# A window-attention block on one core: SyncE's transfers of a step begin only behind the second band's scores of the following step

## The chip, the cores and the metric

One Trainium2 chip, one of its cores. The metric is the time on the device in microseconds (us), the median over runs. The engines are called as in the profile: PE is TensorE's matmul, PEld its weight load, DVE is VectorE, ACT is ScalarE, POOL is GpSimd, SP is SyncE and SPq the queue in which it issues DMAs.

## The reference

A shifted-window attention block with its MLP, all in float32, on x of shape 32 x 56 x 56 x 128 (32 images), with 4 heads of 32 and windows of 7 x 7 tokens:

```
h   = layernorm(x, g1, b1); roll by (-3, -3); cut into 7x7 windows
q, k, v = split(h @ w_qkv + b_qkv)
a   = softmax(q k^T / sqrt(32) + rel_bias + mask)      # per window and head
x   = x + roll_back(unwindow((a v) @ w_proj + b_proj))
out = x + gelu(layernorm(x, g2, b2) @ w_fc1 + b_fc1) @ w_fc2 + b_fc2
```

## The kernel before

**Tiling.** A step is two bands of 7 image rows, 784 tokens, laid out as 112 partitions (two bands of 56 columns) x 7 tiles x 128 channels. An image has 4 steps, so there are 128 steps (`steps`), numbered through. The roll by 3 is done by the DMAs: a step's load is 6 DMAs, and 9 for every fourth step, which wraps round the image's end; its store is the same number of DMAs. `x_in` and `stream` in SBUF have 4 slots (STEPS), and step k uses slot k % 4. `x_in` holds the loaded x. `stream` holds the running result of the step: POOL first writes x plus the projection's bias into it (`add_row` with `x_in`, signal `x_biased`), DVE adds the projection (`residual_added`), POOL adds the second MLP bias, DVE adds the MLP's product in two halves (`out_added[0]`, `out_added[1]`), and SyncE stores it.

**The order is written out by hand.** Each engine runs its own program, a function `step(n)` called for n from -3 to 129 (`run_steps`). One call of it works on several steps of the data at once: in PE's `step(n)` are the projection of n, the scores of n+1 (band 0 near its beginning, band 1 in its middle), most of the MLP of n-1 and its product with w_fc2, the transposes of the first layer norm of n+2, the transposes of the second layer norm xn2 of n, and the attention product of n+1. Engines take their instructions strictly in this order and are tied by semaphores; `upto(k)` is the count that a semaphore with one signal per step has once step k is done, and at most the count of the last step, so `wait(sp, scores_made[1], upto(n + 1))` asks for the scores of the second band of step n+1. A wait for a count of zero or less is left out.

**The pieces around the change.**
- SyncE's `step(n)` (L282 to L293): the load of step n+4 into the slot of step n, after `x_biased` and both halves of `xn1_ready` of n, then the store of step n-2, after both halves of `out_added` of n-2. Loads of steps 0 to 3 and of the weights stand ahead of the loop.
- POOL's `step(n)` (L324 to L343), in this order: normalise the probabilities of n-1, both bands (L314); second MLP bias of n-2 (L321, on `stream`); the power for the first layer norm of n+2 (`rstd1`, L318); x plus bias of n+1 (L321, from `x_in`), which waits for the load of n+1 and for the store of n-3, whose slot it writes over; the power for the second layer norm of n-1 (`rstd2`, L318).
- DVE's `step(n)` (L601 to L661): ...; bias, maximum and shift of the scores of n, band 1, once `scores_made[1]` of n is signalled (L568 to L573); row sums of band 0; then xn2 of n-1, first half (L553, needs `rstd2`); `out_added[0]` of n-2 (L587); row sums of band 1; `out_added[1]` of n-2; the split of x2T and the second half of xn2; the statistics of x of n+3 (L532, needs its load); and more.
- PE's `step(n)` (L768 to L866): `make_scores(1)` of n+1 at L808 signals `scores_made[1]` (L690); then transposes, `make_out(0)`, `make_q`, `make_out(1)` (L763); then the wait for `out_added[0]` of n-1 and the transposes of xn2 of n (L695), and the rest of the step.

Of the kernel before, what the change touches and what calls it, by code (L numbers as in the profile page):

```python
# [42 lines left out]
def wait(eng, sem, value):  # L43

    if value > 0:
        eng.wait_ge(sem, value)

def swin_block(nc, x, g1, b1, w_qkv, b_qkv, w_proj, b_proj, rel_slices, g2, b2, w_fc1, b_fc1, w_fc2,
# [4 lines left out]
    def has(k):  # L53

        return 0 <= k < steps

    def upto(k):

        return min(k, steps - 1) + 1

    def run_steps(step):
        for n in range(-LEAD, steps + LAG):
            step(n)

    with ExitStack() as ctx:
# [92 lines left out]
        def sems(name, n=2):  # L158
            return [sem(f"{name}{i}") for i in range(n)]
# [32 lines left out]
        scores_made = sems("scores_made")  # L192
# [37 lines left out]
        def token_pieces(s, dram, img, tile):  # L230

            pieces = []
            for band in range(BANDS):
                row = STEP_ROWS * s + WIN * band + SHIFT
                whole = min(WIN, ROWS - row)
                for first, t0, t1 in ((row, 0, whole), (0, whole, WIN)):
                    if t0 < t1:
                        rows = dram[img, first * COLS:(first + t1 - t0) * COLS, :].rearrange("(t p) c -> p t c", p=COLS)
                        for col, p, n in ROLLED:
                            p += COLS * band  # L240
                            pieces.append((rows[col:col + n, :, :], tile[p:p + n, t0:t1, :]))
            assert len(pieces) == LOADS[s]
            return pieces

        def dma_count(s, img):

            return img * (16 * LOADS[s]) + 16 * LOADS[s]

        def load_rel(eng, half):

            eng.wait_ge(rel_cleared, 1)
            for ni in range(WIN):
                p, i0 = HALF * half + WIN * ni, WIN - 1 - ni
                eng.dma_start(rel[p:p + WIN, :, :],
                              rel_slices[:, half, :, i0:i0 + WIN, :].rearrange("q h i j -> q h (i j)")).then_inc(rel_loaded, 16)
# [3 lines left out]
        @block.sync  # L259
        def _(sp):  # L260
            def load(img, s):
                for src, dst in token_pieces(s, x, img, x_in[:, s, :, :]):
                    sp.dma_start(dst, src).then_inc(x_loaded[s], 16)

            def store(img, s):
                for dst, src in token_pieces(s, out, img, stream[:, s, :, :]):
                    sp.dma_start(dst, src).then_inc(out_stored[s], 16)

            load(0, 0)
            for dst, src in ((wqkv[:, :], w_qkv), (vecs[:, 0:1], g1), (vecs[:, 1:2], b1), (vecs[:, 2:3], g2),  # L270
                             (vecs[:, 3:4], b2), (bqkv[:, :], b_qkv), (wproj[:, :], w_proj),
                             (wfc1_raw[:, :], w_fc1), (bfc1[:, :], b_fc1),
                             (wfc2[:, :, :], w_fc2.rearrange("(k p) n -> p k n", p=C)),
                             (brow_proj_in[:, :], b_proj.to_broadcast([TOK, C])),
                             (brow_fc2[:, :], b_fc2.to_broadcast([TOK, C])),
                             (mask_sb[:, :, :, :], mask)):
                sp.dma_start(dst, src).then_inc(weights_loaded, 16)
            load_rel(sp, 0)
            for s in range(1, STEPS):
                load(0, s)  # L280

            def step(n):  # L282
                if has(n) and has(n + STEPS):

                    wait(sp, x_biased, upto(n))
                    wait(sp, xn1_ready[0], upto(n))
                    wait(sp, xn1_ready[1], upto(n))
                    load((n + STEPS) // STEPS, n % STEPS)
                if has(n - 2):

                    wait(sp, out_added[0], upto(n - 2))
                    wait(sp, out_added[1], upto(n - 2))
                    store((n - 2) // STEPS, (n - 2) % STEPS)  # L293

            run_steps(step)

            for s in range(STEPS):
                sp.wait_ge(out_stored[s], dma_count(s, images - 1))
# [621 lines left out]
```

## Time and profile before

| | |
|---|---|
| median of 3 runs | 3122.12 us (3111.51 to 3128.21) |
| the profiled execution | 3099.51 us, its span 3097.7 us |
| busy share PE / DVE / ACT / POOL | 97% / 90% / 74% / 42% |
| mean granted clock of TensorE | 0.992 |
| SyncE's transfers | 104.14 MB on queue q1, 13.2% of 16 DMA engines' time |
| SyncE's longest wait in total | for DVE's stream L587 (out_added), 2391.3 us in 128 waits |

The table is read as shares of one long span in which nearly all steps are alike; what sets the time of a step has to be read from the timeline of one of them. The granted clock is a share of 2.4 GHz: 1.00 is that level and 0.50 is 1.2 GHz.

### The profile page before, as it was taken

What the parts mean: (1) busy time and instruction counts of PE and PEld (TensorE: products, weight loads), DVE (VectorE), ACT (ScalarE), POOL (GpSimd) and SP (SyncE); (2) the same over time, 40 slices, a digit from 0 to 9 for tenths busy, and PEclk for the clock granted to TensorE, in tenths of its full rate; (3) what the DMA queues carried; (4) which work ended last, traced back from release to release, by engine and by line L of the source; (5) the groups of instructions that cost most, each with busy time, mean ns of one, the idle gap of its engine ahead of it and who ended that gap; (6) DMA issues with size and microseconds to landing.
All of it is one profiled execution on the core that took longest, in us unless ns stands there. A gap on an engine that the chain in (4) does not pass through costs nothing.

```text
span 3097.7 us, 119627 instructions
## 1 busy us (share of the span) xinstructions
PE 3003.0 (97%) x51984; PEld 2725.4 (88%) x51984; DVE 2803.2 (90%) x7463; ACT 2305.0 (74%) x4482; POOL 1306.6 (42%) x775
## 2 busy tenths in 40 slices
PE   5999999999999999999999999999999999999998
PEld 3898888989988898998899889988999888998897
DVE  7899988999989899999999999989999899999994
ACT  4777777777777777777777777777777777777774
POOL 2444444444434444444444444444444344444442
PEclk8999999999999999999999999999999999999999
DMA  1111111111111111111111111111111111111100
GB/s 55 34 34 34 44 34 34 33 44 34 34 33 44 34 34 35 43 34 33 44 33 34 40 37 34 36 41 34 34 39 39 33 34 39 39 33 37 41 18 22
DMA packets 217572, 111.81 MB, mean 36 GB/s; under 512 B 15094, under 2 KB 216790, under 8 KB 217046
## 3 DMA queue, kind: packets, MB, share of 16 engines
q1 hardware_dynamic: 216899, 104.14, 13.2%
q8 instruction: 408, 6.68, 0.9%
q14 instruction: 118, 0.97, 0.1%
q10 hardware_dynamic: 147, 0.02, 0.0%
HBM read 52.73 MB, written 51.38 MB: 34 GB/s over the span
## 4 chain that ended last, share of the span: by engine, by line
PE 59%; DVE 38%; issue 2%; ACT 0%; SPq 0%; DMA 0%; POOL 0%; POOLq 0%; ACTq 0%; DVEq 0%
PE psum L721 11%; DVE xn L553 9%; PE psum L722 7%; PE psum L723 7%; PE psum L688 7%; DVE row_sum L580 7%; PE psum L742 7%; PE psum L749 6%; PE psum L716 6%; DVE stream L587 4%; DVE scores L568 4%; DVE row_max L571 4%; DVE scores L573 4%; PE psum L703 4%; PE psum L695 3%; DVE x2T_lo L598 2%
## 5 line engine op out<-in xcount | busy, mean ns | idle before, releaser
L763 PEld LDWEIGHTS psum<-wfc,hT 128*112 128x112 f32 x7168 | 806.1, 177 | 39.2 <-issue 21.5
L763 PE MATMUL psum<-wfc,hT 128*112 128x128 f32 x7168 | 824.1, 273 | 1.5 <-ACT hT L407 1.5
L407 ACT ACTIVATE hT<-psum,bias_h 128x392 f32<-128x392 f32 x1024 | 578.8, 594 | 314.6 <-PE psum L723 301.7
L318 POOL TENSOR_TENSOR rstd<-ve,minus_half 112x7 f32<-112x7 f32 x256 | 381.1, 1489 | 986.7 <-DVE ve L548 986.7
L314 POOL TENSOR_TENSOR probs<-probs,row_inv 128x784 f32<-128x784 f32 x256 | 388.7, 1519 | 689.8 <-DVE row_inv L582 689.8
L553 DVE TENSOR_SCALAR xn<-stream,mean,rstd 112x128 f32<-112x128 f32 x896 | 460.4, 571 | 1.6 <-POOL rstd L318 1.6
L587 DVE TENSOR_TENSOR stream<-psum,stream 112x512 f32<-112x512 f32 (+1 forms) x512 | 305.6, 606 | 169.7 <-PE psum L749 153.0
L721 PE MATMUL psum<-x2T_hi,wfc_hi 128*128 128x392 f32 x1024 | 405.0, 395 | 9.2 <-DVE x2T_lo L598 2.0
L722 PE MATMUL psum<-x2T_hi,wfc_lo 128*128 128x392 f32 x1024 | 351.9, 344 | 12.4 <-issue 12.4
L723 PE MATMUL psum<-x2T_lo,wfc_hi 128*128 128x392 f32 x1024 | 351.9, 344 | 0.0
L394 ACT ACTIVATE qd<-psum,bias_q,parity_one 128x392 f32<-128x392 f32 x512 | 316.9, 669 | 3.3 <-PE psum L723 3.3
L321 POOL TENSOR_TENSOR stream<-stream,brow_fc 112x896 f32<-112x896 f32 x128 | 269.0, 2102 | 93.5 <-DVE xn L553 93.5
L721 PEld LDWEIGHTS psum<-x2T_hi,wfc_hi 128*128 128x128 f32 x1024 | 193.5, 189 | 106.5 <-DVE x2T_lo L598 87.4
L695 PE MATMUL psum<-ident,xn 112*128 112x112 f32 x1792 | 271.3, 268 | 10.6 <-DVE xn L553 9.1
L568 DVE TENSOR_TENSOR scores<-psum,bias_rel 128x784 f32<-128x784 f32 x256 | 247.2, 966 | 34.3 <-PE psum L688 34.2
L321 POOL TENSOR_TENSOR stream<-x_in,brow_proj 112x896 f32<-112x896 f32 x128 | 270.3, 2112 | 0.5 <-DMA out<-stream 0.5
L742 PE MATMUL psum<-wv,xT 128*113 128x128 f32 x2048 | 265.4, 272 | 0.0
L573 DVE TENSOR_TENSOR scores<-scores,row_max 128x784 f32<-128x784 f32 x256 | 249.5, 975 | 8.7
L571 DVE TENSOR_REDUCE row_max<-scores 128x16 f32<-128x784 f32 x256 | 248.3, 970 | 8.8
L353 ACT ACTIVATE probs<-scores 128x784 f32<-128x784 f32 x256 | 223.7, 874 | 42.5 <-DVE scores L573 41.1
L361 ACT ACTIVATE probsT<-psum 128x452 f32<-128x452 f32 x512 | 252.0, 550 | 0.6 <-PE psum L703 0.6
L389 ACT ACTIVATE x2T_hi<-psum 128x448 fp32r<-128x448 f32 (+1 forms) x256 | 127.5, 498 | 166.7 <-PE psum L695 166.6
(78 smaller groups left out, 5663.2 us busy)
## 6 DMA issues: line engine op xcount, KB each, us to landing
x_in<-in_x SPq DMA_DIRECT2D x224, 168.0 KB
out<-stream SPq DMA_DIRECT2D x224, 168.0 KB
x_in<-in_x SPq DMA_DIRECT2D x224, 17.5 KB
out<-stream SPq DMA_DIRECT2D x224, 17.5 KB
x_in<-in_x SPq DMA_DIRECT2D x224, 10.5 KB
out<-stream SPq DMA_DIRECT2D x224, 10.5 KB
x_in<-in_x SPq DMA_DIRECT2D x32, 96.0 KB
out<-stream SPq DMA_DIRECT2D x32, 96.0 KB
```

What stands on the lines that cost most here:

```text
L314: pool.tensor_tensor(p, p, r.unsqueeze(2).to_broadcast([128, 2 * WINDOWS, N]), ALU.mult).then_inc(probs_normed[band], 1)
L318: pool.tensor_tensor(rstd[:, :], ve[:, :], minus_half[:, :], ALU.pow).then_inc(ready, 1)
L321: pool.tensor_tensor(stream[:, k % STEPS, :, :], src[:, k % STEPS, :, :], row[:, :].unsqueeze(1).to_broadcast([TOK, TILES, C]), ALU.add).t ...
L407: act.activation(hT[:, chunk, band * BAND:(band + 1) * BAND], tok_psum(c)[:, 0:BAND], ACT.Gelu, bias=bias_h[:, chunk:chunk + 1]).then_inc( ...
L553: last = dve.tensor_scalar(dst[:, t, :], src[:, t, :], mean[:, t:t + 1], rstd[:, t:t + 1], ALU.subtract, ALU.mult)
L573: dve.tensor_tensor(rows, rows, mx.unsqueeze(2).to_broadcast([128, 2 * WINDOWS, N]), ALU.subtract).then_inc(scores_shifted[band], 1)
L587: dve.tensor_tensor(s, tok_psum(h)[0:TOK, 0:(t1 - t0) * C], s, ALU.add).then_inc(ready[h], 1)
L721: pe.matmul(made, w_hi, x_hi, start=True, stop=False)
L722: pe.matmul(made, w_lo, x_hi, start=False, stop=False)
L723: return pe.matmul(made, w_hi, x_lo, start=False, stop=True)
L742: last = pe.matmul(qkvo_psum(V_BANK[band])[0:rows, pair * C:(pair + 1) * C], windows[:, 0:rows], wv[:, :], start=True, stop=True)
L763: last = pe.matmul(tok_psum(h)[0:TOK, (t - t0) * C:(t - t0 + 1) * C], hT[:, chunk, t * TOK:(t + 1) * TOK], wfc2[:, chunk, :], start=chunk ...
```

## The change

SyncE gets one more wait at the head of its `step(n)`, ahead of the load's waits and of the store's. It stands there in every call, whether the call issues something or not. All other engines' programs, the DMAs and the buffers are as before.

```diff
             def step(n):
+                wait(sp, scores_made[1], upto(n + 1))
                 if has(n) and has(n + STEPS):
 
                     wait(sp, x_biased, upto(n))
```

## Rows read from the trace of the kernel before

**Rows 1.** The page's first part: busy us, share of the span, instructions.
```profile
PE 3003.0 (97%) x51984; PEld 2725.4 (88%) x51984; DVE 2803.2 (90%) x7463; ACT 2305.0 (74%) x4482; POOL 1306.6 (42%) x775
```

**Rows 2.** Timeline, PE, one step: start us, us, engine, line, operation [idle before].
```profile
1509.48 0.95 PE L688 MATMUL psum<-kT,qd 64*49 64x49 f32 x64
...
1517.49 0.60 PE L695 MATMUL psum<-ident,xn 112*128 112x112 f32 x4
...
1533.18 0.95 PE L688 MATMUL psum<-kT,qd 64*49 64x49 f32 x64
```

**Rows 3.** Timeline, POOL and DVE in the same step.
```profile
1504.67 2.11 POOL L321 TENSOR_TENSOR stream<-x_in,brow_proj 112x896 f32<-112x896 f32 x1
...
1510.29 1.49 POOL L318 TENSOR_TENSOR rstd<-ve,minus_half 112x7 f32<-112x7 f32 x1 [3.51 <-DVE ve L548]
...
1514.56 2.27 DVE L553 TENSOR_SCALAR xn<-stream,mean,rstd 112x128 f32<-112x128 f32 x4
...
1516.76 0.68 DVE L587 TENSOR_TENSOR stream<-psum,stream 112x512 f32<-112x512 f32 x1
...
1520.72 1.44 DVE L532 BATCH_NORM_STATS2 raw<-x_in 112x6 f32<-112x128 f32 x7
```

**Rows 4.** Timeline, POOL: the bias add of steps 4, 5 and 126.
```profile
103.64 2.11 POOL L321 TENSOR_TENSOR stream<-x_in,brow_proj 112x896 f32<-112x896 f32 x1
...
126.93 2.11 POOL L321 TENSOR_TENSOR stream<-x_in,brow_proj 112x896 f32<-112x896 f32 x1
...
2990.26 2.11 POOL L321 TENSOR_TENSOR stream<-x_in,brow_proj 112x896 f32<-112x896 f32 x1
```

**Rows 5.** Timeline, SyncE's queue: two steps' stores (L267) and loads (L263).
```profile
1495.79 3.29 SPq L267 DMA_DIRECT2D out<-stream  x9
1499.18 2.13 SPq L263 DMA_DIRECT2D x_in<-in_x  x6
1519.09 2.27 SPq L267 DMA_DIRECT2D out<-stream  x6
1521.47 3.18 SPq L263 DMA_DIRECT2D x_in<-in_x  x9
```

**Rows 6.** Timeline near the end: a store, and the bias add behind it.
```profile
3004.66 3.27 SPq L267 DMA_DIRECT2D out<-stream  x9
...
3009.06 2.39 POOL L321 TENSOR_TENSOR stream<-x_in,brow_proj 112x896 f32<-112x896 f32 x1 [0.51 <-DMA out<-stream]
```

**Rows 7.** Windows: us, busy of PE, PEld, DVE, ACT, POOL, PEclk, DMA share, GB/s.
```profile
1502.50:1503.00 0.50, 0.50 (x5) 0.49 (x4) 0.43 (x5) 0.50 (x2) 0.00 (x0) 1.00 0.08 13
```

**Rows 8.** Windows near the beginning, columns as before.
```profile
40.00:42.00 2.00, 0.28 (x1) 0.28 (x2) 1.93 (x3) 1.67 (x4) 0.00 (x0) 0.50 0.00 0
```

**Rows 9.** Timeline, PE, near the beginning.
```profile
41.72 1.68 PE L728 MATMUL psum<-xT,wqk 128*128 128x392 f32 x2 [5.50 <-ACT vs L403]
```

**Rows 10.** Timeline, PE, two gaps inside otherwise steady work.
```profile
410.81 0.41 PE L716 MATMUL psum<-probsT,vs 49*32 49x49 f32 x12 [2.96 <-issue]
...
411.96 0.53 PE L723 MATMUL psum<-x2T_lo,wfc_hi 128*128 128x392 f32 x1
...
909.69 0.38 PE L716 MATMUL psum<-probsT,vs 49*32 49x49 f32 x4 [2.81 <-issue]
```

**Rows 11.** Timeline, POOL: the bias adds around these two gaps.
```profile
411.55 2.09 POOL L321 TENSOR_TENSOR stream<-x_in,brow_proj 112x896 f32<-112x896 f32 x1
439.25 2.11 POOL L321 TENSOR_TENSOR stream<-x_in,brow_proj 112x896 f32<-112x896 f32 x1
...
910.51 2.10 POOL L321 TENSOR_TENSOR stream<-x_in,brow_proj 112x896 f32<-112x896 f32 x1
939.51 2.11 POOL L321 TENSOR_TENSOR stream<-x_in,brow_proj 112x896 f32<-112x896 f32 x1
```

**Rows 12.** Timeline, PE's weight loads in the step of rows 2.
```profile
1519.60 0.19 PEld L721 LDWEIGHTS psum<-x2T_hi,wfc_hi 128*128 128x128 f32 x1 [0.68 <-DVE x2T_lo L598]
...
1522.97 1.27 PEld L716 LDWEIGHTS psum<-probsT,vs 49*32 49x32 f32 x128 [0.33 <-issue]
```

## The prediction

> **What bounds the kernel now.** I read the page's busy line first: TensorE is busy for 97% of the span, DVE for 90% [rows 1]. Neither has room to make up for much, so anything that holds either of them once per step may be paid in full. Then I read the timeline of one step in the middle of the run, and there the order at a single point matters. PE makes the second band's scores and ends them at 1509.48 + 0.95 = 1510.43 [rows 2]; it goes on with other work and starts the transposes of xn2 at 1517.49, with no idle time noted before them. DVE normalises xn2 from 1514.56, with no idle time before it, and adds the first half of the finished step to the stream at 1516.76 + 0.68 = 1517.44, which is what those transposes wait for (out_added[0]) [rows 3]. The reader is to see that DVE reaches this point 0.05 us before PE needs it: whatever makes DVE's xn2 late makes PE late by as much. The steady step is 126.93 - 103.64 = 23.29 us, and over the 122 steps from 103.64 (slot work of step 4) to 2990.26 (step 126) the mean is 2886.62 / 122 = 23.66 us [rows 4]; the 0.37 us between them are PE's stalls for which the profile names "issue" and steps such as the two discussed below.
>
> **What the change moves.** In SyncE's step n the new wait comes before all else. It asks for the second band's scores of step n+1, made in the middle of PE's step n. Behind it on SyncE stand the load of n+4 and the store of n-2. In the trace of before that same store (the one that follows a finished out_added[1]) goes out at 1495.79 and the load behind it at 1499.18, while the scores that the new wait asks for end at 1510.43 [rows 2, 5]. The store thus moves from 1495.79 to behind 1510.43, and a load now stands ahead of it, since the step's load precedes its store.
>
> Who waits for these two? The load feeds x statistics. With the scores of step n+1 made at 1510.43, the load of n+4 is issued by about 1513.7; its first consumer is DVE's statistics at 1520.72 [rows 3], which will themselves be later. The load is hidden, with over 5 us to spare against any landing in the rows. The store feeds POOL. POOL's step n+1 waits for the store of n-2 before it writes x plus the bias of n+2 over the same stream slot, the operation at 1504.67 (2.11 us); the next one in POOL's order is rstd2 at 1510.29 (1.49 us) [rows 3]. And DVE waits for that rstd2 before it normalises xn2, in the same step in which it used the very scores the new wait names. So the order is now forced: scores made, load issued, store issued, store landed, POOL's bias add, POOL's rstd2, DVE's xn2, DVE's out_added[0], PE's transposes. Before, the bias add was over 3.6 us before the scores were (1506.78 against 1510.43) and hid behind everything. Behind the bias add on POOL are also the two normalisations of the probabilities, but these need DVE results that come after or together with xn2, so they keep their distance to it.
>
> **The sum of one step**, from the end of the scores to the start of DVE's xn2. SyncE released, 0.10 (an estimate: nearest is the gap of 0.11 between its store and its load below, in which it passes three waits that are already met). The load's 6 issues, 2.13; in one step of four there are 9, 3.18. Gap to the store, 0.11 (1519.09 + 2.27 to 1521.47). The store's 6 issues, 2.27; one step in four 9, 3.29 [rows 5]. From the end of the issues to POOL's start, 1.13: at the tail, the only place where POOL does wait for a store today, the 9 issues end at 3004.66 + 3.27 = 3007.93 and POOL starts at 3009.06 [rows 6]. Bias add, 2.11, and rstd2, 1.46 more (its 1.49 begins 0.03 before the other's end) [rows 3]. DVE's start, 0.05. Sum 0.10 + 2.13 + 0.11 + 2.27 + 1.13 + 2.11 + 1.46 + 0.05 = 9.36 us for 6 + 6 issues. Loads of 9 go with stores of 6 and the reverse, so two steps in four have 15 issues: about 10.38 us. The mean is 9.87. Before, the same stretch was 1514.56 - 1510.43 = 4.13 us [rows 2, 3]. The stall is 5.2 or 6.3 us, **mean 5.74**.
>
> Does anything take it back? DVE has nothing else to do meanwhile, its queue is in order; and PE has work until about 1517.5 and then nothing, its queue is in order too. From xn2's start on, DVE's and POOL's work has the same relative times as before, and PE's from 1517.49 to the next scores' end at 1533.18 + 0.95 = 1534.13 is nearly solid [rows 2]. I book nothing back. The first store stands in step 2 and POOL first waits for it for slot 4's bias add, the last for 127's: **124 stalls**, 124 x 5.74 = 712 us. The start and the end of the run stay as they are: after the last scores the new wait is already met, and the weights' loads are ahead of it.
>
> The uncertain terms: the landing. The lowest that rows allow is 1.13; a load of 6 issued from 1499.18 to 1501.31 still shows a DMA share of 0.08 between 1502.50 and 1503.00, so 1.7 is the upper end [rows 5, 7]; that would add 0.57 x 124 = 70 us. I take the row where POOL really waited, 1.13. DMA: Bandwidth & Descriptors, in the section Anatomy of one DMA — SWDGE (gpsimd) path of the Trainium skill, gives a fixed cost of about 2.0 us per DMA, mostly the receipt of the write; that path is not SyncE's, but counted from the last issue's start it would put the landing near the upper end and my time some 70 us up, an estimate.
>
> **The clock.** PE will now sit idle for 5.2 to 6.3 us in each step. The trace has short and long gaps of PE to price this by. PE waited 5.50 us ahead of 41.72, and the granted clock is 0.50 there, the 1.2 GHz level [rows 8, 9]. Even a gap of 2.96 us in the middle of solid work (ahead of 410.81) was followed by matmuls of 0.53 us, and that step took 439.25 - 411.55 = 27.70 us: 4.41 over 23.29, of which 2.96 less the usual 0.33 is the gap, so the clock cost 1.8 us [rows 10 to 12]. The gap of 2.81 ahead of 909.69 made its step 939.51 - 910.51 = 29.00: 5.71 over, less 2.48, so 3.2 us. Both gaps are half of what is coming; I therefore expect the low clock after every stall. Bounds are nothing and 3.2 us; of the cost some is absorbed, because right behind the transposes PE has waits for DVE and POOL that would shrink (one is the weight load's 0.68 us for x2T_lo [rows 12]). I take **1.6 us**, a little below the smaller of the two prices. 124 x 1.6 = 198 us.
>
> Total: 712 + 198 = 910 us on the profiled time of 3099.51, 4010 us. The median of the runs is 22.6 us above the profiled one, so the forecast against it is 3122 + 910 = 4032, rounded to **4030 us**, 29% slower. The step should be 23.66 + 7.34 = 31.0 us.
>
> **Rivals.**
> (a) The stall is there but the clock stays at 2.4 GHz, or its loss is wholly absorbed: 3122 + 712 = 3834 us. For it: the waits behind the transposes. Against it: gaps half as long were enough to bring the clock down. TensorE: Matmul & The Clock Gate, HAM oscillation — how this bites in real kernels, in the Trainium skill, describes a loop in which one DMA wait per pass throttles the array anew each time and half of the throttled time is lost; by it this rival is out. By that rule the trace agrees for a single gap, the one ahead of 410.81 [rows 10]; a gap in every step no row of before shows.
> (b) The clock costs as much as in the dearer of the two cases, 3.2 us, every time: 3122 + 712 + 397 = 4231 us. For it: PE resumes with a mix of short work and waits. Against: absorption.
> (c) Only a part of the stall reaches PE, because some of PE's later waits vanish with it or the POOL operations run faster beside an idle DVE: half of 712 and no clock, about 3480 us. Against: no idle time of PE in [rows 2] that depends on anything ahead of the stall.
> (d) The other side: the store's delay is still covered, and moving the DMA traffic away from the stretch of the attend matmuls takes PE's stalls "issue" away (such as the 0.33 us ahead of L716 [rows 12]). At most the 0.37 us per step between 23.66 and 23.29 would go: 3122 - 122 x 0.37 = 3077 us. It decides only if the chain from the store to rstd2 ends before DVE asks for it at 1514.56, so the store would have to have landed by 1514.56 - 3.6 = 1511.0, half a microsecond behind the scores. It can do that only if the new wait is met earlier than I read it, that is, if it asked for scores of a step already past; by the same misreading the change would do nothing.
> (e) The load, not the store, is late and stops DVE at its statistics. That needs a landing over 10 us after the scores plus the stall itself. No row is near; it would add to the time, not replace the stall. I give it no chance of its own.
>
> **How the numbers follow.** Forecast 0.60 (its own range 3940 to 4120, from landing 1.13 to 1.7 and clock 1.2 to 1.9), (a) 0.15, (b) 0.17, (c) 0.05, (d) with "nothing changes" 0.03. The range 3840 to 4220 leaves out (c), (d) and the outer parts of (a) and (b). Faster by over 0.5% has 0.015, within 0.5% (about what a measurement of this kernel can tell) 0.015, slower 0.97.
>
> **What the changed profile would show.** SyncE's waits lead with PE's scores L688 as releaser instead of DVE's stream L587. SyncE's timeline has load and store back to back, 12 or 15 issues, once per step, just behind the second scores. POOL's bias add L321 waits for DMA out<-stream some 124 times, and the distance from the scores' end to it is about 6 to 7 us. DVE's xn L553 on the stream waits for rstd L318, 5 to 6 us a time; PE's transposes L695 wait for DVE's stream L587 about as long. The granted clock falls to some 0.85 or less on the mean. The bias-add period is about 31 us. Wrong would be: L553 without a wait (then (c) or (d)), a granted clock near 0.99 (then (a)), or statistics L532 waiting for the load (then (e)).

## The result and the profile after

| | median us | lowest and highest of 5 runs |
|---|---|---|
| before | 3122.12 | 3111.51 to 3128.21 |
| changed | 4138.76 | 4130.57 to 4147.73 |
| ratio | 1.3285 | 95% interval 1.3243 to 1.3328 |

The changed kernel takes 1017 us more, a third. The forecast was 4030 us with a range of 3840 to 4220.

The page of the changed kernel begins as follows (busy time by engine, then the chain that ended last). The added line moves all line numbers behind it up by one, so L689 here is L688 before, L322 is L321, L554 is L553.

```profile
PE 3257.6 (79%) x51984; PEld 2982.0 (72%) x51984; DVE 2801.9 (68%) x7463; ACT 2338.7 (56%) x4482; POOL 1295.2 (31%) x775
...
PE 56%; SPq 14%; POOL 11%; DVE 10%; DMA 6%; issue 4%; ACT 0%; POOLq 0%; ACTq 0%; DVEq 0%
```

DVE's busy time is the same as in [rows 1] to within 2 us and POOL's is 11 us less, so neither got more work. PE is busy 255 us longer with the same 51984 instructions: that is a slower clock, not work. And the chain that ended last now runs through SyncE's queue, POOL and the DMAs for 31% of the span; in the kernel before, the page gives each of them 0% of it.

The waits, in total, and SyncE's own (engine, line <- what it waited for: us, times, longest):

```profile
POOL stream L322 <- DMA out<-stream: 1661.6, 124, 18.6
...
DVE xn L554 <- POOL rstd L319: 796.1, 126, 8.0
PE psum L696 <- DVE stream L588: 790.7, 125, 8.0
```
```profile
SPq L263 <- PE psum L689: 3264.0, 123, 31.3
```

POOL's bias add waits for the store 124 times, the number counted in the prediction, and the two waits behind it have the same size, 790.7 / 125 = 6.33 us each: what DVE loses for rstd2, PE loses for DVE. The 1661.6 us of POOL are longer because POOL comes to its wait early; they are not the price.

One step of the changed kernel, the same instructions as in [rows 2] and [rows 3] (timeline: start us, us, engine, line, operation, idle before it; SyncE's queue and POOL's among them, lines of other work left out):

```profile
2005.43 0.95 PE L689 MATMUL psum<-kT,qd 64*49 64x49 f32 x64
...
2006.44 2.13 SPq L263 DMA_DIRECT2D x_in<-in_x  x6
...
2008.67 3.56 SPq L267 DMA_DIRECT2D out<-stream  x9
...
2013.36 2.07 POOL L322 TENSOR_TENSOR stream<-x_in,brow_proj 112x896 f32<-112x896 f32 x1 [12.70 <-DMA out<-stream]
2015.38 1.49 POOL L319 TENSOR_TENSOR rstd<-ve,minus_half 112x7 f32<-112x7 f32 x1
...
2016.91 2.30 DVE L554 TENSOR_SCALAR xn<-stream,mean,rstd 112x128 f32<-112x128 f32 x4 [6.31 <-POOL rstd L319]
2019.14 0.68 DVE L588 TENSOR_TENSOR stream<-psum,stream 112x512 f32<-112x512 f32 x1
...
2019.87 1.01 PE L696 MATMUL psum<-ident,xn 112*128 112x112 f32 x4 [6.28 <-DVE stream L588]
```

Read it as a staircase. The scores end at 2006.38, SyncE issues 0.06 us later, load and store are out at 2012.23, POOL starts 1.13 us behind, DVE gets its rstd2 at 2016.87, PE its go at 2019.82. Each step of the stair begins within 0.1 us of the end of the one above but for the landing. From the scores' end to DVE's xn2 there are 10.53 us, where there were 4.13.

The four transposes that end the list are listed with 1.01 us; the same ones take 0.60 in [rows 2]. The clock around them (windows: length, busy PE, PEld, DVE, ACT, POOL, PEclk, DMA share, GB/s):

```profile
2018.00:2020.00 2.00, 0.13 (x1) 0.13 (x2) 2.00 (x6) 0.00 (x0) 0.36 (x1) 0.50 0.00 0
2020.00:2022.00 2.00, 2.00 (x12) 2.00 (x13) 1.86 (x4) 0.87 (x2) 0.95 (x1) 0.50 0.00 0
2022.00:2024.00 2.00, 2.00 (x7) 1.37 (x6) 2.00 (x9) 1.02 (x3) 1.32 (x2) 0.53 0.00 0
2024.00:2026.00 2.00, 2.00 (x21) 1.97 (x20) 0.53 (x3) 1.81 (x4) 1.35 (x1) 1.00 0.00 0
```

PE sat idle, and when it resumed the granted clock stood at 0.50, the 1.2 GHz level, for about 4 us of full work. The clock records show a stretch at the lower level in each of 120 steps counted from xn2 to xn2, where the kernel before has one in 5 of 120; the mean clock of the span is 0.876 against 0.992.

The period of the bias add, to be set beside [rows 4] (steps 4 and 126, 122 steps apart):

```profile
118.61 2.07 POOL L322 TENSOR_TENSOR stream<-x_in,brow_proj 112x896 f32<-112x896 f32 x1 [13.05 <-DMA out<-stream]
...
4038.50 2.08 POOL L322 TENSOR_TENSOR stream<-x_in,brow_proj 112x896 f32<-112x896 f32 x1 [9.83 <-DMA out<-stream]
```

(4038.50 - 118.61) / 122 = 32.13 us, against 23.66: 8.47 us per step. PE's wait for DVE's stream, averaged over the 121 steps that the timeline shows whole, is 6.41 us of it. That leaves 2.06 us, for which the low clock is the suspect. (By the delay of xn2, 10.66 us behind the scores on the mean against 4.13, the stall is 6.53 us and the remainder 1.94: the listed idle time of PE starts at the modelled end of its last matmul, about 0.1 us late. The experiments below go by the listed idle time.)

### The profile page after: what moved, and what is told of

Same layout as the page of the kernel before. It is cut to its first block, busy times and chain, and to the rows that moved or that the text cites. A ratio compares the mean times of both kernels' runs of the same rounds, so it can differ in the third digit from the quotient of the medians.

```text
span 4145.9 us, 119751 instructions
## 1 busy us (share of the span) xinstructions
PE 3257.6 (79%) x51984; PEld 2982.0 (72%) x51984; DVE 2801.9 (68%) x7463; ACT 2338.7 (56%) x4482; POOL 1295.2 (31%) x775
## 4 chain that ended last, share of the span: by engine, by line
PE 56%; SPq 14%; POOL 11%; DVE 10%; DMA 6%; issue 4%; ACT 0%; POOLq 0%; ACTq 0%; DVEq 0%
PE psum L704 8%; PE psum L722 7%; DVE xn L554 7%; SPq L263 7%; SPq L267 7%; POOL stream L322 6%; PE psum L723 6%; PE psum L724 6%; PE psum L689 5%; DMA out<-stream 5%; PE psum L743 5%; PE psum L696 5%; PE psum L750 5%; POOL rstd L319 4%; PE psum L717 4%; PE psum L729 4%
## 5 line engine op out<-in xcount | busy, mean ns | idle before, releaser
L554 DVE TENSOR_SCALAR xn<-stream,mean,rstd 112x128 f32<-112x128 f32 x896 | 438.9, 546 | 795.7 <-POOL rstd L319 795.7
L696 PE MATMUL psum<-ident,xn 112*128 112x112 f32 x1792 | 321.6, 305 | 800.6 <-DVE stream L588 790.7
L696 PEld LDWEIGHTS psum<-ident,xn 112*128 112x128 f32 x1792 | 223.8, 162 | 834.5 <-DVE stream L588 815.8
L322 POOL TENSOR_TENSOR stream<-x_in,brow_proj 112x896 f32<-112x896 f32 x128 | 265.0, 2070 | 1661.6 <-DMA out<-stream 1661.6
L722 PE MATMUL psum<-x2T_hi,wfc_hi 128*128 128x392 f32 x1024 | 473.3, 462 | 3.4 <-DVE x2T_lo L599 2.0
L723 PE MATMUL psum<-x2T_hi,wfc_lo 128*128 128x392 f32 x1024 | 364.8, 356 | 9.9 <-issue 9.9
L704 PE MATMUL psum<-ident,probs 113*128 113x113 f32 x2048 | 363.3, 344 | 2.2 <-POOL probs L315 2.2
L724 PE MATMUL psum<-x2T_lo,wfc_hi 128*128 128x392 f32 x1024 | 363.4, 355 | 0.0
L704 PEld LDWEIGHTS psum<-ident,probs 113*128 113x128 f32 x2048 | 335.1, 198 | 12.4 <-POOL probs L315 3.7
L729 PE MATMUL psum<-xT,wqk 128*128 128x392 f32 x512 | 296.9, 673 | 9.9 <-ACT vs L404 7.9
L362 ACT ACTIVATE probsT<-psum 128x452 f32<-128x452 f32 x512 | 270.2, 550 | 61.1 <-PE psum L704 59.8
L322 POOL TENSOR_TENSOR stream<-stream,brow_fc 112x896 f32<-112x896 f32 x128 | 268.3, 2096 | 93.4 <-DVE xn L554 93.4
```

The source lines that it names most:

```text
L322: pool.tensor_tensor(stream[:, k % STEPS, :, :], src[:, k % STEPS, :, :], row[:, :].unsqueeze(1).to_broadcast([TOK, TILES, C]), ALU.add).t ...
L554: last = dve.tensor_scalar(dst[:, t, :], src[:, t, :], mean[:, t:t + 1], rstd[:, t:t + 1], ALU.subtract, ALU.mult)
L696: last = pe.transpose(tok_psum(h)[:, (t - t0) * TOK:(t - t0 + 1) * TOK], src[:, t, :], ident[0:TOK, 0:TOK])
L704: last = pe.transpose(psum[:, S_BANK + 2 * band + f, 128 * pair:128 * pair + rows], probs[0:rows, band, f, 2 * pair:2 * pair + 2, :].rearr ...
L722: pe.matmul(made, w_hi, x_hi, start=True, stop=False)
L723: pe.matmul(made, w_lo, x_hi, start=False, stop=False)
```

## Experiments

The theory to be tested: the store lands late, POOL's in-order queue puts rstd2 behind the bias add that waits for it, DVE and PE lose 6.4 us, and the idle PE loses its clock for another 2 us. Its rivals: the load is what comes late; a wait in SyncE's queue, or the meeting of its traffic with other work, costs by itself; the remainder of 2 us is not the clock.

**1. The store ahead of the load, behind the same wait.**

```diff
                 wait(sp, scores_made[1], upto(n + 1))
-                (load of n+4) (store of n-2)
+                (store of n-2) (load of n+4)
```

> The changed kernel with the store placed ahead of the load behind the same wait. Theory (store landing, POOL's bias add, rstd2, DVE's xn2, PE): the load's issues leave the chain, 2.57 + 0.11 = 2.7 us per step of the changed kernel, so the stall falls from 6.4 to about 3.7 us and the time to 4139 - 124 x 2.7 = 3805 us, less if the clock falls more rarely. Rival (the load is what arrives too late): it now goes out later, so no gain or a loss, 4139 us or more.

Measured: 3805.19 us, ratio 1.2197 (1.2146 to 1.2247). From the waits:

```profile
DVE xn L554 <- POOL rstd L319: 453.6, 126, 4.6
PE psum L696 <- DVE stream L588: 447.8, 125, 4.5
```

The time is the expected one. The load, issued later still, made nothing slower, and the stall fell by 2.81 us, to 3.60 us on the mean: the load's issues and the gap behind them took 2.64 us of the chain, and the store's own issues take 0.16 us less when no load stands right ahead of them. The period is 29.23 us, so what is left over the stall, 29.23 - 23.66 - 3.60 = 1.97 us, is as large as with the longer gap. A gap of 3.6 us costs as much clock as one of 6.4. The clock records show why: the time at the lower level falls from some 1030 us in the changed kernel to 667, but the part of it in which PE has work hardly changes, 622 and 598 us. What the longer gap adds at the low clock is time in which PE is idle anyway.

**2. Only the load gated; the store goes out ahead of the wait.**

```diff
+                (store of n-2)
                 wait(sp, scores_made[1], upto(n + 1))
                 (load of n+4)
-                (store of n-2)
```

> Only the load stands behind the new wait, the store goes out ahead of it as before. Theory: nothing waits for the load, so the time is that of the kernel before, 3122 us within 0.5%. Rival (the late load stalls DVE's statistics, or the wait's place or the meeting of load traffic with other work costs by itself): over 3200 us.

Measured: 3104.36 us, ratio 0.9959 (0.9936 to 0.9982). The load as the culprit is out: it is delayed as in the changed kernel and costs nothing. Whether the 0.4% is a gain is taken up in 7 and 8.

**3. PE kept busy in its wait, twice.** Behind the last of the MLP's product and ahead of the wait for out_added[0], PE gets matmuls whose result nothing reads, in columns of a PSUM bank that nothing uses. They are added work, the rest is computed as before.

```diff
+            def fill(count):
+                for _ in range(count):
+                    pe.matmul(psum[:, QKVO_BANK + 1, BAND:512], ident[:, :], wfc2[:, 0, 0:512 - BAND], start=True,
+                              stop=True)
...
                     make_out(1)
                 if has(n):
+                    if n >= 2:
+                        fill(44)
                     wait(pe, out_added[0], upto(n - 1))
```

> The changed kernel with 44 idle matmuls (120 columns into columns of a PSUM bank that nothing reads) ahead of PE's wait for out_added[0], from step 2 on: some 5 us of work that fits into the wait of 6.4 us, so the gap is about 1.3 us. The stall itself stays. Theory (of the 8.4 us per step 6.4 are the stall and 2.0 the low clock behind it): the mean granted clock goes to 0.97 or more and the time to about 4139 - 124 x 2.0 = 3890 us. Rival (the remainder is not the clock but other waits): 4139 us or, for the added work, more.

Measured: 4303.78 us, ratio 1.38 (1.375 to 1.3851), clock 0.99. I had sized the filler wrongly: the 44 took 9.98 us instead of some 5, more than the gap, so PE no longer waited at all and its own filler became the bound. The run says that the clock stays up when PE has work, and nothing of the price. With half as many:

> The changed kernel with 22 idle matmuls ahead of PE's wait for out_added[0]. With 44 they took 9.98 us, more than the wait, so 22 take 5.0 us and fit into the wait of 6.4 us, leaving a gap of 1.4 us. The stall itself stays. Theory (6.4 us per step are the stall, 2.0 us the low clock behind it): mean granted clock 0.97 or more, 4139 - 124 x 2.0 = 3890 us. Rival (the remainder over the stall is not the clock): 4139 us.

Measured: 3942.13 us, ratio 1.2661 (1.2623 to 1.2698), clock 0.982. In the timeline (each of the 22 matmuls is recorded as two instructions):

```profile
2010.22 5.07 PE L762 MATMUL psum<-wfc,ident 128*128 128x120 f32 x44
...
2016.86 0.60 PE L696 MATMUL psum<-ident,xn 112*128 112x112 f32 x4 [1.57 <-DVE stream L588]
```

DVE's wait for rstd2 is unchanged (789.8 us against 796.1), so the stall is the same, filled with useless work; the transposes are back at 0.60 us, and the kernel is 197 us faster for it. Per step, by the period of the bias add, 32.13 - 30.45 = 1.68 us. As the clock has two levels, 1.00 and 0.50, the time at the lower one is twice the missing share of the span: 2 x 0.124 x 4145.9 = 1028 us in the changed kernel, 2 x 0.018 x 3947.0 = 142 us here, 2 x 0.008 x 3097.7 = 50 us in the kernel before. So at least 1.7 of the 2.06 us are the clock, and 30.45 - 23.66 - 6.40 = 0.39 us per step are left. The same trace says what they are. Counted from xn2 to xn2, 93 of 120 steps have no time at the low level; their period is 30.00 us and DVE's wait for rstd2 6.46, which leaves 23.54 us, against 23.47 in the 115 such steps of the kernel before. The other 27 steps take 31.96 us. The remainder is thus the clock that still fell in these, and 0.39 x 124 = 48 us of it are nearly all of the 52 us by which the time is above the expected one.

**4. POOL's bias add one step later, out of the way of rstd2.**

```diff
             (POOL, step(n))
                 if has(n - 2):
                     wait(pool, xn2_ready[1], upto(n - 2))
                     add_row(n - 2, stream, brow_fc2, x1_biased)
+                if has(n):
+                    wait(pool, x_loaded[n % STEPS], dma_count(n % STEPS, n // STEPS))
+                    if has(n - 4):
+                        wait(pool, out_stored[n % STEPS], dma_count(n % STEPS, (n - 4) // STEPS))
+                    add_row(n, x_in, brow_proj, x_biased)
                 (rstd1 of n+2)
-                (the same for n + 1, with its two waits)
                 (rstd2 of n-1)
             (DVE, step(n))
                     wait(dve, proj_made[0], upto(n))
+                    wait(dve, x_biased, upto(n))
                     add_to_stream(n, 0, residual_added)
```

> The changed kernel, but POOL adds x and the bias of a step one step later, behind the second bias add, so that neither rstd2 nor the probabilities stand behind the wait for the store; DVE gets a wait for x_biased ahead of the first half of the projection. Theory: the store has landed 5 us or more before POOL asks for it, nobody waits, 3122 us within 1%. Rival (the late transfers cost by traffic or through another consumer): over 3200 us.

Measured: 3133.81 us, ratio 1.0051 (1.0027 to 1.0074). The wait of POOL for the store is gone from the waits, and with it all but 0.5% of the loss, though SyncE's transfers are as late as in the changed kernel, the load 0.06 us behind the scores' end at 1504.81:

```profile
1503.86 0.95 PE L690 MATMUL psum<-kT,qd 64*49 64x49 f32 x64
...
1504.87 2.13 SPq L263 DMA_DIRECT2D x_in<-in_x  x6
1507.10 2.43 SPq L267 DMA_DIRECT2D out<-stream  x6
```
```profile
1517.48 2.11 POOL L322 TENSOR_TENSOR stream<-x_in,brow_proj 112x896 f32<-112x896 f32 x1
```

The bias add begins 7.95 us after the store is out (1509.53) and with no idle time. This is the whole mechanism undone at its narrow place, not at SyncE. The control is the same edit on the kernel before:

> The kernel before with POOL's later bias add alone: the control for the changed kernel with it. Theory: nobody waits for that operation in either, so this is 3122 us within 1% and equal to the other (3134 us) within 0.5%. Rival (the changed order of SyncE costs some of the 14 us there): below 3120 us.

Measured: 3137.16 us, ratio 1.0072 (1.0046 to 1.0099), the same as with the change within 0.1% by the medians and 0.2% by the ratios. So the 0.5 to 0.7% belong to POOL's new order, and with that order SyncE's new wait costs nothing that can be measured. The two traces agree: their steps without low clock take 23.67 and 23.71 us, where those of the kernel before take 23.47.

**5. The wait on the first band's scores, 5.0 us earlier.**

```diff
-                wait(sp, scores_made[1], upto(n + 1))
+                wait(sp, scores_made[0], upto(n + 1))
```

> The changed kernel with the wait on the first band's scores of the same step, which end 5.0 us earlier. Theory: the chain from the scores to DVE's xn2 starts 5.0 us earlier, so of the mean stall of 6.4 us 1.4 us are left (1.1 for 12 issues, 1.7 for 15), the gap is too short to bring the clock down each time, and the time is 3122 + 124 x 1.4 = 3298 us. Rival (any wait in the middle of PE's step costs most of the loss): over 3600 us; rival (slack I have not seen): 3122 us.

Measured: 3450.92 us, ratio 1.1079 (1.1041 to 1.1116). Two thirds of the loss are gone, but the number is 153 us above my expectation. The waits:

```profile
POOL stream L322 <- DMA out<-stream: 1046.0, 124, 12.5
...
PE psum L696 <- DVE stream L588: 250.7, 125, 3.1
```

The stall is 250.7 / 125 = 2.0 us, not 1.4, because the chain from the first band's scores to xn2 takes 11.3 us here, where the chain behind the second band's took 10.66. POOL's two operations now meet DVE's score arithmetic, and both sides are slower for it:

```profile
1503.27 2.08 POOL L322 TENSOR_TENSOR stream<-x_in,brow_proj 112x896 f32<-112x896 f32 x1 [7.67 <-DMA out<-stream]
1503.39 2.80 DVE L574 TENSOR_TENSOR scores<-scores,row_max 128x784 f32<-128x784 f32 x1
...
1505.31 2.22 POOL L319 TENSOR_TENSOR rstd<-ve,minus_half 112x7 f32<-112x7 f32 x1
```

On the mean rstd2 takes 1.85 us instead of 1.49, the bias add 2.21 instead of 2.07, and DVE's shift of the second band's scores 1.71 instead of 0.97 (that of the first band, which meets neither, stays at 0.97); DVE is thus itself later at xn2 and waits for rstd2 only 159.5 / 124 = 1.3 us. The landing is longer too, 1.86 us on the mean instead of 1.64; why was not tested. And the clock falls in about half of the steps (62 of 120; mean 0.960; 276 us at the low level), which I had ruled out for gaps so short. The period is 26.56 = 23.66 + 2.03 + 0.87. To see whether the 0.87 us are the clock, the same with 8 idle matmuls in the gap:

> The changed kernel with the wait on the first band's scores (3451 us where 3298 was expected), and 8 idle matmuls, some 1.8 us, ahead of PE's wait for out_added[0], which took 2.0 us there. If that miss is a stall of 2.0 instead of 1.4 us plus 0.87 us per step of low clock, the gap all but vanishes, the clock stays up (0.985 or more) and the time is 3451 - 124 x 0.87 = 3343 us. If the miss is anything but the clock: 3451 us.

Measured: 3385.69 us, ratio 1.0867 (1.0838 to 1.0897), clock 0.990: 65 us faster with more work in it. In the trace the period falls by 0.65 us to 25.92. The clock is most of the 0.87 us and not all of it. In the 111 of 120 steps without low clock the period is 25.65 us, 2.18 above the 23.47 of such steps before, where the stall accounts for 2.03: 0.15 us are not clock and weren't separated. The time is 43 us above the expected one.

**6. The wait one step earlier.**

```diff
-                wait(sp, scores_made[1], upto(n + 1))
+                wait(sp, scores_made[1], upto(n))
```

> The changed kernel with the wait on the second band's scores of one step earlier, which are made over 8 us before the store's own wait is met. Theory: the wait instruction costs nothing by itself, 3122 us within 0.5%. Rival (an added wait in SyncE's queue costs by itself): slower by over 1%.

Measured: 3102.22 us, ratio 0.9957 (0.9935 to 0.998). The wait as such is free; its price is the event it names.

**7 and 8. Is there a gain in 2 and 6?** Both came out 0.4% below the kernel before, with intervals clear of 1, and neither had a shorter period in its trace (23.68 and 23.71 us against 23.66). So they were run again beside an unchanged copy of the kernel before.

> The kernel before, unchanged, as the null for the two runs below: a ratio of 1.000, and how far one build of the same program lies from another.

> Only the load behind the new wait, again. The first time it was 0.4% faster with an interval clear of 1, and its period in the trace was the same 23.66 us. If moving the load away helps: 0.996 again. If it was the spread between runs: 1.000, within 0.3%.

> The wait one step earlier, again; also 0.4% faster the first time, though nothing is moved in it. 1.000 within 0.3% if that was spread; 0.996 again if the added wait by itself shifts something.

Measured: the unchanged copy 1.0023 (1.0007 to 1.0039), the gated load 0.9972 (0.9955 to 0.9989), the earlier wait 0.9973 (0.9957 to 0.9989). The copy, which can't differ, differs from itself by 0.2%, beyond its own interval. Against the copy the two are 0.5 and 0.6% lower, against the other runs 0.3%. What differs with the time is the granted clock: its median over the runs is 0.9865 for the copy, 0.988 for the other runs of the kernel before, and 0.9895 and 0.990 for the two. Among the runs of the kernel before alone it goes the same way, 3130.39 us at 0.983 and 3098.64 at 0.991. The steps without low clock take 23.40 us with the gated load and 23.41 with the earlier wait, 23.45 and 23.51 in the first runs of the two, 23.47 and 23.52 in the kernel before and its copy. So a gain of that size can't be told from the spread between runs, which comes with how often the clock falls; what makes it fall more or less often isn't shown. I leave it open. No version was found that clearly beats the kernel before.

## Why the prediction was right

The measured median lies 109 us above the forecast, inside the stated range, but 19 us above the forecast's own narrower range of 3940 to 4120. By the number alone it is nearer to rival (b), 4231, than to 4030, so it is the steps that decide. By the prediction's own steps:

- **DVE reaches its point 0.05 us before PE needs it, so DVE's delay is PE's.** Right: 796.1 us of DVE's waits against 790.7 us of PE's.
- **The load is hidden.** Right: no wait for it in the profile after, and gating it alone costs nothing.
- **The forced order scores, load, store, landing, bias add, rstd2, xn2.** Right, each link in the staircase above; cutting it at SyncE's order took away the load's share, cutting it at POOL took away all.
- **124 stalls.** Right, 124 waits.
- **The sum of one step, 9.87 us, stall 5.74.** Too small: 10.66, and a stall of 6.41 by PE's listed idle time or 6.53 by the delay of xn2. The term that was mis-sized is the landing, 1.13 us assumed, 1.65 measured. The one row for it, [rows 6], was a store of 9 DMAs. Behind stores of 9 the landing is 1.19 us in the changed kernel, but behind the stores of 6, three quarters of all, it is 1.8. I had named 1.7 as the upper end and 70 us as its price, and should have asked why it could be longer in the usual case. In a store of 6 the large pieces are nearer to the end of the issues; that this is the reason wasn't tested. The store's issues took 2.76 instead of 2.53 us on the mean of all steps, and the load's 2.53 instead of 2.39. The other terms were within 0.1 us. Together the sum was 0.79 us short.
- **The low clock after every stall, 1.6 us.** The clock fell in all 120 steps counted, to 0.876 on the mean. TensorE: Matmul & The Clock Gate, HAM oscillation — how this bites in real kernels, in the Trainium skill, which the prediction drew on, has one wait per pass bring the clock down each time; the trace agrees. It also has half of the time at the low level lost, and there the trace does not agree: 2.06 x 124 = 255 us are a quarter of some 1030, since PE had work in only 622 of them. The price of 1.9 to 2.06 us per step is 0.3 to 0.46 us above the term.
- **The rest.** 8.47 us per step in the profiled executions, 1017 / 124 = 8.2 by the medians, where 7.34 were forecast. The two terms account for the difference of 1.13: 0.67 for the stall and 0.46 for what stands behind it, or 0.79 and 0.34 by the delay of xn2. Both terms were too small, so no errors cancelled.

The rivals: (a), stall without loss of clock, is excluded by the filler, which saved 197 us; (b), 3.2 us of clock each time, by the 2.06 us that are all there is. (c) fails because PE lost all that DVE lost. (d), no loss or a gain, needed the wait to be met early; with the wait really one step earlier the loss is gone, which shows the reading of its index to be the point. (e) fell with the gated load.

## What to carry to other kernels

The price of a wait that is added on one queue is found by following what that queue feeds until it meets an engine with no slack: here SyncE's store let POOL's bias add go, and only the instruction behind that one in POOL's order was urgent. When an in-order engine has an operation with room of a whole step in front of an urgent one, the room is not the operation's own, and moving it behind the urgent one (at 0.5 to 0.7% here) protects the kernel from a late transfer. And when a stall makes TensorE idle in each pass, book the slower clock behind it as a term of its own.

## What the runs showed of the hardware that was not expected

- The clock's price does not grow with the gap: gaps of 6.4 and 3.6 us cost 2.06 and 1.97 us per step. Gaps of 2.0 us still brought the clock down in about half of the steps, for 0.65 us per step by the filler. The stretch at the low level is longer behind the longer gap, but PE has work in about as much of it (622 of some 1030 us, and 598 of 667).
- Useless matmuls in a gap can make a kernel faster: 22 per step gave 4138.76 to 3942.13 us, 8 per step 3450.92 to 3385.69. They only help if they fit; 44, at 0.23 us each, made it 4303.78.
- Where POOL's operations overlap DVE's shift of the scores, all are slower. The bias add takes 2.07 us while DVE is idle, 2.11 beside its usual work and 2.21 on the mean in experiment 5; rstd2 takes 1.49 us elsewhere and 1.85 there, DVE's shift 0.97 and 1.71, in single steps 2.8 to 2.9.
- From the last issue of a store to the start of the engine that waits for it there were, in the changed kernel, 1.19 us after 9 DMAs and 1.8 us after 6, of the same number of bytes.
